# Last batch through masked 32-row groups, experts summed on VectorE, a semaphore per first load, new orders

## The chip, the cores and the metric

The kernel runs on one core of one Trainium2 chip. The metric is the device time in microseconds of one execution. Engines: PE (TensorE), DVE (VectorE), ACT (ScalarE), POOL (GpSimd), and SP (SyncE), which here issues the DMAs.

## The reference, cut to what matters

Eight batches of 256 tokens with 128 features pass four residual stages, each behind a layer norm:

```
x += tanh(g_xattn[0]) * attention(LN(x), ctx; 8 heads of 64, 512 keys) @ Wo + bo        stage X
x += tanh(g_ffn[0]) * (self-attention(LN(x); 16 heads of 8, 256 keys)
                       + top-2 of 8 experts, softmax gates, with biases)                stage F
x += tanh(g_xattn[1]) * attention(LN(x), ctx; 16 heads of 8, 512 keys) @ Wo + bo        stages K (keys, values), B
x += tanh(g_ffn[1]) * sum over top-2 experts of (x We + prob) * weight                  stage C
```

## The kernel before

Every batch is the same list of steps, named stage, step, batch, part. Stage X: xin and ctx (loads), ls, rs, xh (the norm: statistics on DVE, power on POOL, scaling on DVE), ln (transposes), kp, qp, vp (projections), mx (8 score fills, whose maxima DVE reduces), mT (the maxima as a row), e (8 exponent fills: scores again, minus the row maximum, exp on ACT), pv (times values), dn and dT (denominators), out (projection by Wo), xs (POOL sums the heads). Stages F and B, with heads of 8 rows: qk (projection), sp (POOL splits each f32 into three bf16 parts), sw and sr (the parts go to DRAM and come back restacked, 48 rows for each head, two heads side by side in row halves 0 to 63 and 64 to 127), mx8 (maxima; 8 fills for F, 16 for B), mT8, mw and mr (the maxima go through DRAM too, as a 49th row), e8 (8 and 16 fills), pv8, oT, and for B aT and out8 (Wo). F and C also have gate, gx (top 2 and weights w), moe (4 fills of 512 columns, times w on DVE, added up on POOL) and fin (POOL); the bias part of F is wT, wb. C ends with out, the store.

A fill is a PE step into one or two of eight PSUM banks that ACT or DVE then drains. The planner, `schedule()` (lines 256 to 322), lists all steps with costs and what they depend on, and chooses one greedily at a time by EARLY x start time + a wanted time (`AMOUNTS`, lines 51 to 93). Its result is `ORDER`, one fixed sequence for each engine; each engine executes its own, and waits on semaphores. `MODE` puts PE steps in groups that split the array alike; a change of group has a cost in the plan. `WARMERS` is a number of filler matmuls that the planner puts ahead of a PE step where it expects PE to idle (line 596: ident times wqx). `L...` in a profile is a line of this file.

What the change touches: the first loads (list `first`, line 499, one semaphore w_first of 8 x 16; awaited by PE at line 586, by ACT ahead of the Tanh at 757, by POOL at 1014); the 19 later loads (`loads`, semaphore w_loaded); the DVE memset of PSUM (833); POOL's memsets of k8 and v8 (1013); the steps of batch 7 in F, K, B and C; the planner. Lines that the prediction names: 601 ln, 605 qp, 609 kp, 620 and 706 scores for mx and mx8, 636 and 640 e, 649 pv, 667 out, 725 e8, 737 pv8, 693 moe on PE and 980 on DVE, 1069 to 1077 moe on POOL, 1085 to 1093 fin, 902 xh, 1027 and 1028 rs, 949 oT, 875 w.

Of the kernel before, what the change touches and what calls it, by code (L numbers as in the profile page):

```python
# [50 lines left out]
EARLY, SWITCH, PERIOD = 297.1242, 52.68, 114.223  # L51
AMOUNTS = {
# [13 lines left out]
    ("DVE", "C", "gate"): (273.74, -377.36), ("DVE", "C", "gx"): (98.96, 88.96), ("DVE", "C", "moe"): (-499.91, -524.03),  # L66
    ("POOL", "X", "rs"): (-116.96, 345.46), ("POOL", "X", "xb"): (-243.12, -152.43), ("POOL", "X", "e"): (82.49, 251.41),
    ("POOL", "X", "xs"): (114.49, -8.85), ("POOL", "F", "rs"): (162.64, -182.35), ("POOL", "F", "sp"): (-2.47, 375.02),
    ("POOL", "F", "moe"): (162.93, -42.41), ("POOL", "F", "fin"): (62.3, 335.36), ("POOL", "K", "sp"): (367.67, -161.62),
    ("POOL", "B", "rs"): (64.61, 155.9), ("POOL", "B", "xb"): (99.7, -174.62), ("POOL", "B", "sp"): (6.72, -89.93),  # L70
    ("POOL", "C", "rs"): (-194.63, 117.07), ("POOL", "C", "moe"): (290.04, 342.6), ("POOL", "C", "fin"): (650.19, -128.95),
# [1057 lines left out]
```

## Time and profile before

| | us |
|---|---|
| median of 3 runs | 736.36 (733.67 to 737.97) |
| the profiled execution | 737.18 |
| its span, first to last instruction | 735.3 |
| mean granted TensorE clock | 0.984 |
| PE, DVE, ACT, POOL busy | 649.0, 520.3, 401.1, 401.2 |

The span is what the rows below cut up; the profiled execution took 1.9 us more. Busy time is a union over instructions, and says of PE only that something was in the array, fillers included. A row of the timeline has start, duration, engine, line, operation, written tile and read tiles, and in brackets the idle time before it with what ended it.

### The profile page before, as it was taken

How to read it: one execution, taken by the hardware profiler on the slowest of the kernel's cores; microseconds unless marked ns; L12 is line 12 of the kernel's file. 1: busy time of each engine (PE TensorE's matmuls, PEld its weight loads, DVE VectorE, ACT ScalarE, POOL GpSimd, SP SyncE). 2: the span in 40 equal slices, each digit the busy share in tenths (PEclk: the TensorE clock that was granted, in tenths of full speed). 3: DMA queues.
4: the chain of work that ended last, by engine and by line, in shares of the span. 5: the costliest groups of instructions: out<-in, count | busy, mean ns of one | idle time of the engine just before them, and what ended most of it. 6: DMA issues, size and time to landing. Idle time of an engine off the chain costs nothing.

```text
span 735.3 us, 14119 instructions
## 1 busy us (share of the span) xinstructions
PE 649.0 (88%) x5616; PEld 338.8 (46%) x5616; DVE 520.3 (71%) x993; ACT 401.1 (55%) x562; POOL 401.2 (55%) x551
## 2 busy tenths in 40 slices
PE   3998997899899999999999998999999897897882
PEld 1564453554345533554454544554364444343541
DVE  2607557698758787897869787897778658958513
ACT  2463547456845675458655784558543861573350
POOL 7275784771575567628565566636663685040234
PEclk9999999999999999999999999999999999999898
DMA  6130324410060045102350046104420434210000
GB/s 184 40 71 18 75 44 65 98 45 2 9 139 3 12 95 104 44 12 68 78 98 2 20 95 115 28 14 86 89 48 12 89 81 111 44 45 8 2 8 8
DMA packets 64369, 40.62 MB, mean 55 GB/s; under 512 B 5032, under 2 KB 62320, under 8 KB 64304
## 3 DMA queue, kind: packets, MB, share of 16 engines
q1 hardware_dynamic: 64304, 39.72, 25.2%
q8 instruction: 44, 0.72, 0.4%
q14 instruction: 21, 0.17, 0.1%
HBM read 22.80 MB, written 16.91 MB: 54 GB/s over the span
## 4 chain that ended last, share of the span: by engine, by line
PE 54%; DVE 21%; POOL 8%; ACT 8%; issue 5%; DMA 2%; SPq 1%; POOLq 0%; DVEq 0%
PE psum L737 9%; PE psum L649 8%; PE psum L636 7%; DVE mx8B L992 7%; DVE mxA L917 3%; ACT probB L825 3%; PE psum L706 3%; PE psum L609 3%; PE psum L725 3%; PE psum L693 3%; PE psum L614 2%; ACT probX L806 2%; PE psum L700 2%; PE psum L640 2%; PE psum L596 1%
## 5 line engine op out<-in xcount | busy, mean ns | idle before, releaser
L992 DVE TENSOR_REDUCE mx8B<-psum 128x2 f32<-128x1024 f32 x128 | 148.3, 1215 | 13.7 <-PE psum L706 13.2
L825 ACT ACTIVATE probB<-psum 128x1024 f32<-128x1024 f32 x128 | 125.7, 1026 | 18.1 <-PE psum L725 17.6
L917 DVE TENSOR_REDUCE mxA<-psum 128x2 f32<-128x1024 f32 x64 | 76.7, 1217 | 35.2 <-PE psum L620 35.0
L806 ACT ACTIVATE probX<-psum 128x1024 f32<-128x1024 f32 x64 | 65.4, 1026 | 49.0 <-PE psum L640 48.7
L987 DVE TENSOR_REDUCE mx8F<-psum 128x4 f32<-128x1024 f32 x64 | 75.8, 1219 | 11.0 <-PE psum L700 10.0
L636 PE MATMUL psum<-qA,kA 64*128 64x256 f32 x512 | 76.9, 393 | 0.6 <-ACT mrow L779 0.5
L825 ACT ACTIVATE probF<-psum 128x1024 f32<-128x1024 f32 x64 | 63.4, 1023 | 16.9 <-PE psum L725 16.0
L1048 POOL TENSOR_TENSOR sums<-sums,probX 128x512 f32<-128x512 f32 x32 | 40.6, 1270 | 56.8 <-ACT probX L806 55.5
L737 PE MATMUL psum<-probB,v8B 128*9 128x256 f32 x1024 | 64.1, 393 | 4.6 <-ACT probB L825 2.8
L649 PE MATMUL psum<-probX,vX 128*64 128x256 f32 x512 | 62.1, 385 | 2.4 <-ACT probX L806 2.4
L706 PE MATMUL psum<-k8B,q8B 48*128 48x512 bf16 x256 | 47.2, 388 | 12.0 <-DVE mx8B L992 6.9
L1045 POOL TENSOR_TENSOR sums<-probX 128x512 f32<-128x512 f32 x32 | 40.6, 1268 | 19.2 <-ACT probX L806 19.1
L725 PE MATMUL psum<-q8B,k8B 49*128 49x256 bf16 x512 | 47.2, 274 | 3.0 <-ACT probB L825 2.0
L636 PEld LDWEIGHTS psum<-qA,kA 64*128 64x128 f32 x512 | 40.0, 189 | 17.8 <-issue 3.1
L649 PEld LDWEIGHTS psum<-probX,vX 128*64 128x64 f32 x512 | 34.0, 136 | 25.7 <-ACT probX L806 7.0
L1069 POOL TENSOR_TENSOR prodC<-prodC 128x256 f32<-128x256 f32 x32 | 23.3, 727 | 41.2 <-DVE prodC L980 41.0
L609 PE MATMUL psum<-cTX,wkx 96*128 96x512 f32 x64 | 34.5, 665 | 10.9 <-DMA wvx<-in_wvx 10.9
L1049 POOL TENSOR_TENSOR sums<-sums,probX 128x512 f32<-128x512 f32 x32 | 40.7, 1271 | 2.5
L737 PEld LDWEIGHTS psum<-probB,v8B 128*9 128x9 f32 x1024 | 25.6, 92 | 34.8 <-issue 6.1
L725 PEld LDWEIGHTS psum<-q8B,k8B 49*128 49x128 bf16 x512 | 17.5, 94 | 50.4 <-ACT probB L825 16.0
L1053 POOL TENSOR_TENSOR sums<-sums 128x512 f32<-128x512 f32 x16 | 20.3, 1268 | 33.5 <-DVE sums L926 33.5
L737 PE MATMUL psum<-probF,v8F 128*9 128x256 f32 x512 | 33.6, 380 | 3.7 <-ACT probF L825 2.7
(203 smaller groups left out, 1262.3 us busy)
## 6 DMA issues: line engine op xcount, KB each, us to landing
k8B<-k_dK SPq DMA_DIRECT2D x16, 384.0 KB, 6.0
k_dK<-partsK SPq DMA_DIRECT2D x8, 384.0 KB, 2.6
q8F<-q_dF SPq DMA_DIRECT2D x16, 192.0 KB, 4.5
k8F<-k_dF SPq DMA_DIRECT2D x16, 192.0 KB, 5.1
q8B<-q_dB SPq DMA_DIRECT2D x16, 192.0 KB, 3.8
k_dK<-partsK SPq DMA_DIRECT2D x8, 256.0 KB, 2.9
cTX<-in_ctxT SPq DMA_DIRECT2D x8, 192.0 KB, 2.7
cTK<-in_ctxT SPq DMA_DIRECT2D x8, 192.0 KB, 3.1
```

The source lines that it names most:

```text
L609: last = mm(ps[:, j * KV:(j + 1) * KV], wkx[:, (2 * k + j) * P:(2 * k + j + 1) * P], cT["X"][:], start=True, stop=True)
L636: mm(ps[:, 512 * i + SEQ * c:512 * i + SEQ * (c + 1)], kA[half_i, h, (2 * f + c) * P:(2 * f + c + 1) * P], qA[half_i, h, :], start=True, s ...
L649: last = mm(ps[64 * i:64 * i + 64, 0:SEQ], vX[:, c, h * XD:(h + 1) * XD], prob[s][(2 * k + c // 2) % SLOTS[s]][:, o:o + SEQ], start=(c == ...
L706: last = mm(ps[:, KV * i:KV * (i + 1)], q8[s][b % TURNS[s]][64 * i:64 * i + KROWS, p, t * P:(t + 1) * P], k8[s][b % TURNS[s]][64 * i:64 * ...
L725: last = mm(ps[:, 512 * i + SEQ * c:512 * i + SEQ * (c + 1)], k8[s][b % TURNS[s]][64 * i:64 * i + MROWS, p, (c0 + c) * P:(c0 + c + 1) * P] ...
L737: last = mm(ps[32 * i:32 * i + D8 + 1, 0:SEQ], v8[s][:, c, h, :], prob[s][(NPAIR * KEYS[s] // SEQ * b + u) % SLOTS[s]][:, o:o + SEQ], star ...
L806: nc.scalar.activation(prob[s][k % SLOTS[s]][:], ps, ACT.Exp, scale=float(XD) ** -0.5).then_inc(done["ACT"], 1)
L825: nc.scalar.activation(prob[s][(units * b + k) % SLOTS[s]][:], ps, ACT.Exp, scale=float(D8) ** -0.5).then_inc(done["ACT"], 1)
L917: nc.vector.tensor_reduce(mxA[:, t, h:h + 65:64], ps.rearrange("p (i n) -> p i n", i=2), AX.X, ALU.max, negate=True).then_inc(drained, 1)
L987: nc.vector.tensor_reduce(mx8[s][:, :, 2 * k:2 * k + 2].rearrange("p t i -> p i t"), ps.rearrange("p (i t n) -> p i t n", i=2, t=QT), AX.X ...
L992: nc.vector.tensor_reduce(mx8[s][:, t, 2 * p:2 * p + 2], ps.rearrange("p (i n) -> p i n", i=2), AX.X, ALU.max, negate=True).then_inc(drain ...
L1049: engine.tensor_tensor(sums[:, h], sums[:, h], p[:, :, 1, :], ALU.add).then_inc(S["X"]["psum"], 1)
```

## The change

1. First loads. wkx, ident and the gates are issued from ACT's queue, the rest from SP's, with a semaphore for each of ident, wkx, wqx, wvx, wox, graw and bo. Each step waits for what it reads. PE starts with 4 filler matmuls on mxA, once the first PSUM bank is cleared. The memsets of k8 and v8 become a planned POOL step `sets`; at its end it waits for w_loaded (20 loads now) and multiplies the masks with two biases. The bias scaling and pick become steps too (`bo`, `pick`).
2. Batch 7 of F and B. No split, no DRAM. The weights of the projections are loaded into wqx and wkx (`tw`). q is masked by head, so that of each group of 32 rows only 8 rows of one head are not zero; k stays as it is. tmx multiplies groups of 32 rows in bf16 for the maxima; tmT transposes these; te multiplies in f32, plus a bf16 product that subtracts the maxima, as e of stage X does. tpv, oT as before with heads in another sequence. qk becomes tqb (DVE, 4 masked copies), tqf (ACT, 4) and tkb (ACT, 2). POOL clears the tiles for it (`tset`).
3. Batch 7 of X: xs of part 1 runs on DVE (txs). Batch 7 of C: DVE multiplies and adds each of 8 experts from the banks (tmoe, 16 operations of 128 columns), POOL adds the bias part to x meanwhile (`tx`), DVE ends with tfin, and each half is stored by itself.
4. `AMOUNTS` and the greedy choice are gone. `TURN_OF` spells the sequence of each engine, a letter for each step (an index into STEPS); `schedule()` only derives banks, waits and fillers from it.

```diff
-START = 13.
+START = {"PE": 5.4, "DVE": 5.2, "ACT": 5.0, "POOL": 1.3, "SP": 9.0}
+EARLY_FILLERS = 4
-EARLY, SWITCH, PERIOD = 297.1242, 52.68, 114.223
-AMOUNTS = {
...
+STEPS = {
...
+    "POOL": (("X", "rs"), ("X", "pick"), ("X", "bo"), ("K", "sets"), ("X", "xb"), ("X", "e"), ("X", "xs"), ("F", "rs"),
...
+TURN_OF = {
+    "PE": "ebaycbdydddxdeddxdafgggghghbgggchihjkdkdbddededlddnmpofpggbgqpghggaphhsgsgssshssbsitcedjkukdurduvudduvueuvldumdv"
...
+    "POOL": "dacebalffffffffggehijfafffjffffjjkggehlimajfnojffjfjffffkggheimjjjjkonfalfpfffffqqfqmggheqriojjfpnffjfjffakfflqq"
...
+def plan_direct(p, s, b, keys, v, old):
+
+    n = KEYS[s] // P
+    units = GROUP * n
+    for k in range(units):
+        p.fill("DVE", 1, s, "tmx", b, k, .22, 1.13, [("DVE", s, "tqb", b, 0), keys], [("POOL", "F", "tset", b, 0)])
+        if k % n == n - 1:
+            p.fill("ACT", 0, s, "tmT", b, k // n, .22, .3, [("DVE", s, "tmx", b, k)], [("POOL", "F", "tset", b, 0)])
...
         @block.sync
-            load_x(0)
             load_ctx("X", 0)
-            for dst, src in first:
-                engine.dma_start(dst, src).then_inc(w_first, 16)
+            load_x(0)
+            engine.dma_start(wqx[:], a["wqx"]).then_inc(loaded["wqx"], 16)
+            engine.dma_start(wvx[:], a["wvx"]).then_inc(loaded["wvx"], 16)
+            for dst, src in bias:
+                engine.dma_start(dst, src).then_inc(loaded["bo"], 16)
+            engine.dma_start(wox[:], a["wox"]).then_inc(loaded["wox"], 16)
             for dst, src in loads:
                 engine.dma_start(dst, src).then_inc(w_loaded, 16)
-            sp.wait_ge(c_set, MEMSETS)
...
         @block.tensor
-            pe.wait_ge(w_first, W_FIRST)
+            pe.wait_ge(c_set, X_SETS)
             pe.wait_ge(ps_set, 1)
+            for _ in range(EARLY_FILLERS):
+                early = mm(psum[:, 0, 0:SEQ], mxA[:, 0, :], mxA[:].rearrange("p t n -> p (t n)"), start=True, stop=True)
...
+                elif name == "te":
+                    j, i, c0 = (k // 2, k % 2, 0) if s == "F" else (k // 4, k // 2 % 2, 2 * (k % 2))
...
+                    for c in range(2):
+                        for g in (2 * i, 2 * i + 1):
+                            o, rows = 512 * (g % 2) + SEQ * c, slice(ROWS * g, ROWS * g + ROWS)
+                            mm(ps[:, o:o + SEQ], keyL[s][rows, (c0 + c) * P:(c0 + c + 1) * P], qA[rows, j, :],
+                               start=True, stop=False, tile_position=(ROWS * g, 0))
+                        for g in (2 * i, 2 * i + 1):
+                            o, rows = 512 * (g % 2) + SEQ * c, slice(ROWS * g, ROWS * g + ROWS)
+                            last = mm(ps[:, o:o + SEQ], onesL[rows], rowL[j][rows], start=False, stop=True, tile_position=(ROWS * g, 0))
...
         @block.vector
+                if name == "tfin":
+                    dve.wait_ge(based, QT)
+                    dve.wait_ge(*is_done("C", "tmoe", b, 2 * k + 1))
+                    nc.vector.scalar_tensor_tensor(out=fin["C"][:, k, :], in0=acc["C"][:, k, :], scalar=gates[:, 3:4],
+                                                   in1=x1["C"][:, k, :], op0=ALU.mult, op1=ALU.add).then_inc(S["C"]["fin"], 1)
...
+                elif name == "tmoe":
...
+                    for e in range(4):
+                        part, weight = ps[:, e * P:(e + 1) * P], w[s][:, t, 4 * f + e:4 * f + e + 1]
+                        if f == 0 and e == 0:
+                            ins = nc.vector.tensor_scalar(acc[s][:, t, :], part, weight, None, ALU.mult)
+                        else:
+                            ins = nc.vector.scalar_tensor_tensor(out=acc[s][:, t, :], in0=part, scalar=weight, in1=acc[s][:, t, :],
+                                                                 op0=ALU.mult, op1=ALU.add)
+                        if e < 3:
+                            link(s, ins)
+                    ins.then_inc(drained, 1)
...
         @block.gpsimd
+                elif name == "sets":
+                    for tile in (*k8["F"], *k8["B"], v8["F"], v8["B"]):
+                        engine.memset(tile[:], 1.0).then_inc(k_set, 1)
+                    pool.wait_ge(w_loaded, W_LOADS)
+                    for to, n in (("F", 0), ("B", 2)):
+                        engine.tensor_scalar(bqm[to][:], mask[:], bqn[:, n:n + 1], None, ALU.mult).then_inc(k_set, 1)
```

The first letters on PE read: e vp, b kp, a ln, y vv of stage K, c qp, b kp, d mx. On POOL: d `sets`, a rs, c `bo`, e xb, b pick.

## Rows read from the trace of the kernel before

**Rows 1.** The page: span, busy time (share) xinstructions, and PE's busy tenths by slice.
```profile
span 735.3 us, 14119 instructions
PE 649.0 (88%) x5616; PEld 338.8 (46%) x5616; DVE 520.3 (71%) x993; ACT 401.1 (55%) x562; POOL 401.2 (55%) x551
...
PE   3998997899899999999999998999999897897882
```
**Rows 2.** Timeline of PE, 574:590: the last output projection of batch 7.
```profile
576.36 1.07 PE L667 MATMUL psum<-wox,oX 64*128 64x128 f32 x16
```
**Rows 3.** Timeline of all engines, 0:30.
```profile
9.98 0.59 POOL L1013 MEMSET v8B<- 128x576 f32 x1
...
10.90 3.78 PE L609 MATMUL psum<-cTX,wkx 96*128 96x512 f32 x4 [10.90 <-DMA wvx<-in_wvx]
...
14.02 0.43 SPq L556 DMA_DIRECT2D weB<-in_weB  x1
14.26 0.23 POOL L1027 TENSOR_SCALAR veX<-mvX 128x2 f32<-128x2 f32 x1
...
15.99 0.69 PE L601 MATMUL psum<-ident,xhX 128*128 128x128 f32 x2 [1.30 <-DVE xhX L902]
...
19.89 2.83 PE L605 MATMUL psum<-xTX,wqx 128*128 128x256 f32 x8
...
24.75 0.61 PE L620 MATMUL psum<-kAb,qAb 64*128 64x512 bf16 x4 [0.31 <-ACT qA L791]
```
**Rows 4.** Windows: length, busy of PE, PEld, DVE, ACT, POOL (x), PEclk, DMA share, GB/s.
```profile
287.70:368.70 81.00, 75.70 (x690) 39.42 (x690) 65.61 (x125) 49.88 (x71) 48.66 (x68) 1.00 0.27 58
...
577.50:647.70 70.20, 59.68 (x522) 30.05 (x518) 54.47 (x121) 34.09 (x52) 31.15 (x53) 1.00 0.38 76
647.70:711.00 63.30, 54.05 (x495) 26.38 (x494) 34.12 (x80) 34.72 (x47) 18.99 (x38) 0.92 0.07 18
```
**Rows 5.** Waits of PE, 287.7:529.6: us in total, times, longest.
```profile
PE psum L601 <- DVE xhB L902: 3.4, 3, 1.1
PE psum L693 <- DVE prodC L980: 3.1, 3, 1.1
```
**Rows 6.** Groups by line of PE, 577.5:711: busy us, mean ns, idle before.
```profile
L596 PE MATMUL psum<-wqx,ident 128*128 128x256 f32 x70 | 19.4, 426 | 2.1 <-DVE x L935 1.0 <-DVE mx8B L992 0.9 <-DVE v8B L960 0.2
```
**Rows 7.** Timeline of all engines, 704:736.
```profile
709.01 1.92 PE L737 MATMUL psum<-probB,v8B 128*9 128x256 f32 x32 [0.32 <-ACT probB L825]
...
712.48 0.29 DVE L949 TENSOR_TENSOR attB<-psum,rrB 128x128 f32<-128x128 f32 x1
...
723.40 0.17 DVE L875 TENSOR_TENSOR wC<-w0C,w1C 128x16 f32<-128x16 f32 x1
...
732.30 0.72 POOL L1093 TENSOR_TENSOR accC<-accC,x 128x256 f32<-128x256 f32 x1
```
**Rows 8.** Windows of 15 to 19 us, columns as in rows 4.
```profile
15.00:16.00 1.00, 0.01 (x1) 0.01 (x1) 0.60 (x2) 1.00 (x2) 0.30 (x1) 1.00 0.40 76
17.00:18.00 1.00, 1.00 (x2) 0.34 (x1) 0.00 (x0) 0.10 (x1) 0.00 (x0) 1.00 1.11 368
...
18.50:19.00 0.50, 0.50 (x1) 0.02 (x1) 0.00 (x0) 0.00 (x0) 0.00 (x0) 1.00 0.13 26
```
**Rows 9.** Timeline of PE, 391:402 and 655:704.
```profile
392.96 0.60 PE L636 MATMUL psum<-qA,kA 64*128 64x256 f32 x4
...
393.51 0.60 PE L636 MATMUL psum<-qA,kA 64*128 64x256 f32 x4
...
394.24 0.39 PE L706 MATMUL psum<-k8B,q8B 48*128 48x512 bf16 x2
394.62 1.95 PE L649 MATMUL psum<-probX,vX 128*64 128x256 f32 x16
396.50 0.39 PE L706 MATMUL psum<-k8B,q8B 48*128 48x512 bf16 x2
396.72 0.38 PE L725 MATMUL psum<-q8F,k8F 49*128 49x256 bf16 x4
...
663.47 3.58 PE L737 MATMUL psum<-probB,v8B 128*9 128x256 f32 x32 [0.30 <-ACT probB L825]
```

More of the change, by code:

```diff
@@ L50 @@
 IDLE, WARM_UP, WARM = .25, .43, True
-EARLY, SWITCH, PERIOD = 297.1242, 52.68, 114.223
-AMOUNTS = {
[13 rows of a table removed]
[L66 to L71, printed above, removed]
[21 rows of a table removed]
+LETTERS = "abcdefghijklmnopqrstuvwxyzABCDEFGHIJKLMNOPQRSTUVWXYZ0123456789"
@@ L157, in plan_gate @@
     for k, us in enumerate(busy):
-        p.job("DVE", s, "gx", b, k, us, ("ACT", s, "gx", b, 0), ("DVE", s, "moe", b - 1, 3), ("POOL", s, "fin", b - 1, 0))
+        p.job("DVE", s, "gx", b, k, us, ("ACT", s, "gx", b, 0), ("DVE", s, "moe", b - 1, 3), ("POOL", s, "fin", b - 1, 0),
+              *([("PE", "F", "wT", b - 1, 0)] if s == "F" else []))
 def plan_moe(p, s, b, last, old):
@@ L224, in plan_c, with turns @@
 def plan_c(p, b):
-    plan_norm(p, "C", b, ("DVE", "B", "out8", b, 0), [("PE", "C", "moe", b - 1, 3)])
+    plan_norm(p, "C", b, [("DVE", "B", "out8", b, 0)], [("PE", "C", "moe", b - 1, 3), ("PE", "C", "gate", b - 1, 0)])
     plan_gate(p, "C", b, (.8, .6, .6, .67))
-    plan_moe(p, "C", b, 3, ("SP", "C", "out", b - 1, 0))
-    p.job("SP", "C", "out", b, 0, .43, ("POOL", "C", "fin", b, 0))
+    if b < LAST:
+        plan_moe(p, "C", b, 3, ("SP", "C", "out", b - 1, 0))
+        p.job("SP", "C", "out", b, 0, .43, ("POOL", "C", "fin", b, 0))
+        return
+    p.job("POOL", "C", "tx", b, 0, 2.4, ("DVE", "C", "gx", b, 3), ("DVE", "C", "xh", b, 0))
+    for k in range(4):
+        p.fill("DVE", 0, "C", "tmoe", b, k, .86, 1.1, [("ACT", "C", "ln", b, 0)], [("DVE", "C", "gx", b, 3), ("SP", "C", "out", b - 1, 0)])
+    for k in range(QT):
+        p.job("DVE", "C", "tfin", b, k, .25, ("DVE", "C", "tmoe", b, 2 * k + 1), ("POOL", "C", "tx", b, 0))
+        p.job("SP", "C", "out", b, k, .43, ("DVE", "C", "tfin", b, k))
 def slack(key):
+    if key in (("SP", "X", "xin", 0, 0), ("SP", "X", "ctx", 0, 0)):
+        return 0.
     return OUT if key[0] == "PE" else LAND[key[1:3]] if key[0] == "SP" else 0.
-def targets(jobs):
-    count = {}
-    for e, s, name, b, k in jobs:
-        count[e, s, name] = max(count.get((e, s, name), 0), k)
-    out = {}
-    for key in jobs:
-        group, b, k = key[:3], key[3], key[4]
-        off, step = AMOUNTS[group]
-        out[key] = PERIOD * b + off + step * (k / count[group] if count[group] else 0.)
-    return out
+def turns(p):
+    groups, order = {}, {}
+    for key in p.jobs:
+        groups.setdefault(key[:3], []).append(key)
+    for e, letters in TURN_OF.items():
+        steps = [groups.pop((e, *group)) for group in STEPS[e]]
+        left = [iter(keys) for keys in steps]
+        order[e] = [next(left[LETTERS.index(letter)]) for letter in letters]
+        assert len(order[e]) == sum(len(keys) for keys in steps)
+    assert not groups
+    return order
 def free_banks(wide, bank_free, now):
@@ L261, in schedule @@
     jobs = {key: (busy, [a for a in after if a in p.jobs]) for key, (busy, after) in p.jobs.items()}
[L262 to L270 removed]
+    turn = turns(p)
+    free, at = dict(START), dict.fromkeys(turn, 0)
     never = 1e9
@@ L322, in schedule, with ready @@
-    return order, bank_of, before, p.drain, over, warm
+    over, before, warm = {}, {}, {}
+    def ready(key):
+        e, after = key[0], jobs[key][1]
+        if any(a not in over for a in after):
+            return None
+        return max([over[a] + HOP * (a[0] != e) for a in after], default=0.)
+    while len(over) < len(jobs):
+        went = False
+        for e in ("SP", "POOL", "ACT", "DVE"):
+            while at[e] < len(turn[e]) and ready(turn[e][at[e]]) is not None:
+                key = turn[e][at[e]]
+                free[e] = max(free[e], ready(key)) + jobs[key][0]
+                over[key] = free[e] + slack(key)
+                at[e] += 1
+                went = True
+                if p.drain.get(key[1:]) == e:
+                    for i in range(BANKS):
+                        if held[i] == key[1:]:
+                            bank_free[i] = over[key] + HOP
+        if went:
+            continue
+        key = turn["PE"][at["PE"]]
+        fill, other = key[1:], MODE.get(key[1:3], 0) != mode
+        start = max(free["PE"] + DRAIN_OUT * other, ready(key))
+        when, banks = free_banks(p.wide[fill], bank_free, start)
+        assert when < never
+        start = max(start, when)
+        idle = start - max(free["PE"], when)
+        warm[fill] = int(min(20, max(0., idle - IDLE) // WARM_UP)) if WARM else 0
+        before[fill] = [held[i] for i in banks if held[i]]
+        bank_of[fill] = banks[0]
+        for i in banks:
+            held[i], bank_free[i] = fill, never
+        free["PE"] = start + jobs[key][0]
+        if other:
+            mode = MODE.get(key[1:3], 0)
+            free["PE"] += ENTRY.get(key[1:3], .1)
+        over[key] = free["PE"] + slack(key)
+        at["PE"] += 1
@@ L325 @@
+    return {e: [key[1:] for key in keys] for e, keys in turn.items()}, bank_of, before, p.drain, over, warm
 ORDER, BANK, FORMER, DRAIN, OVER, WARMERS = schedule()
@@ L689, in _ @@
                         last = mm(ps[:, t * NE:(t + 1) * NE], xT[s][:, t * P:(t + 1) * P], wg[s][:], start=True, stop=True)
[L690 removed]
+                elif name in ("moe", "tmoe"):
                     t, f = divmod(k, 2)
```

415 lines of the change are left out of this document (293 added, 122 removed), and 54 rows, old and new, of tables (AMOUNTS, STEPS).

## The prediction

> **What bounds the kernel now.** The page comes first [rows 1]. TensorE (PE) is busy for 649.0 of 735.3 us, VectorE for 520.3, ScalarE and GpSimd for 401 each. The PE row has two soft ends: nothing in the first slice, and 7s and 8s in the last third. To give them sizes I cut the span at two events: the last matmul of the output projection of batch 7, at 577.4 us, and the last attention-times-value matmul of batch 7, which ends at 710.9 [rows 2, 7]. This gives four stretches.
>
> - Start: PE does nothing until 10.90, where it is released by wvx, last of the eight first loads. The first score matmul starts at 24.75 [rows 3].
> - Middle: three whole periods take 241.9 us, with some 75.6 us of PE work in each (the first is shown, 75.70 in 81.00) [rows 4]. PE is 94% busy, VectorE 81%. The waits that a profile can name sum to 14.0 us in the three periods, and the longest is 1.1 us [rows 5]. So the middle is bound by PE; only those some 5 us of idle per batch can be had there.
> - Tail, 577.5 to 711: 133.5 us, PE "busy" 59.68+54.05=113.7 [rows 4]. But 19.4 of it are filler matmuls that multiply ident by wqx and whose result nobody reads [rows 6]. Real work is 94.3 us, idle and filler 39.2 us. Here the round trips of the last batch through DRAM are no longer covered by other batches.
> - End chain, 711 to 735.3: 24.3 us of one dependent chain, oT, aT, out8, norm, gate, experts, store. From w at 723.57 on it alternates between DVE and POOL until the sum ends at 733.02 [rows 7].
>
> **The change part by part.**
>
> *First loads.* PE, ScalarE and the bias code no longer wait for all eight first loads. One would subtract the 10.9 us. I don't, because of the new GpSimd order: its first letter is d, the step `sets`, ahead of a, the step `rs` of batch 0. `sets` runs the memsets (the last starts at 9.98 before [rows 3]) and then waits for w_loaded, all 20 later loads, to make two masked biases. Queued behind this on POOL is rs, so xh, ln, qp and every score of batch 0 wait for the last weight load. When does it land? weB, the last of them, is issued at 14.02 [rows 3]; the DMA engines are full in 17:18 (1.11) and nearly idle (0.13) from 18.5 on [rows 8]; so the loads are in by about 18.3. In after, weB is SP's 27th issue and not its 29th, at 0.47 us each (29 issues up to 14.02, the first at 0.7): 0.95 us earlier, 17.3. DMA share was only 0.40 at 15:16 [rows 8], so issue, not the rate, sets the time there.
> The Trainium skill ("DMA: Bandwidth & Descriptors", section "Issuing engines are not separate DMA queues") says that issuing from several engines saves only the sequencer's time, because all run on the same 16 DMA engines. By that alone, with saturated engines, nothing lands earlier and the start would be 0.95 us worse than below; the share of 0.40 says that the engines had room.
> From 17.3, with durations of [rows 3]: two small bias operations 0.5, ve and rstd 1.03 (14.26 to 15.29), xh to first transpose 0.65, transposes at the idle clock 0.73 to the start of xT, xT 0.38. That is 20.6. The new PE order puts vv of batch 0 ahead of qp: about 0.7 later; qp 2.83, copies 2.0 (from the end of qp, 22.72, to 24.75): 26.2 against 24.75. kp and vp lie in PE's idle time in both, so the start costs **+1.4**. Bounds: -1 (loads land by 15, nothing ahead of qp) to +3.
>
> *Orders of batches 0 to 6.* Same steps, other sequence. I count mode groups along the PE order as the diff writes it out (groups of MODE): 371 changes of group instead of 339 up to the last output projection. A change costs 0.16: at 394.24 a pair that takes 0.22 elsewhere (396.50 to 396.72) is followed by the other mode only at 394.62 [rows 9]. 32 x 0.16 = +5.1. Against it stands the wait of L693 for prodC, 3.1 us in three periods, about 1.0 per batch [rows 5]. Before, the first three moe fills of C stand next to each other (1, 1 and 12 places apart), while GpSimd still adds up the products of the one before; in the new order they are 3 to 20 places apart. That wait goes: 7 x -1.0 = -7. The wait for xhB (also 1.1 each) stays, since the work between oT and ln of B is as long as before. Sum **-2**. Bounds: all 5 us per batch of idle gone, 6 x -5 + 5 = -25; as much new idle as was saved, +12. I take the small one because only one wait can be shown to go.
>
> *Last batch, attention of F and B.* Removed: the splits on POOL, the stores and loads of parts, maxima through DRAM. With them goes the reason for fillers and idle. Added on PE: each of the 24 exponent units was 4 bf16 matmuls, 0.22 like the score pair from 396.50 on, and is now 4 f32 and 4 bf16, like a unit of X, whose half takes 0.55 (392.96 to 393.51) [rows 9]: 24 x (1.09-0.22) = +20.9. Row transposes and the extra projections +2.2. Mode changes in the tail 111 instead of 82, as 32-row and 64-row units alternate: 29 x 0.16 = +4.6. Real work 94.3+27.7=122. Minus some 4 us (an estimate from the mean clock of 0.92 over 63.30 us) that cold stretches cost before (the 32 matmuls that take 1.92 at 709.01 take 3.58 at 663.47, in a stretch whose granted clock is 0.92 on average, so partly at 1.2 GHz and not 2.4 [rows 4, 7, 9]) = 118. The new order leaves no planned filler in the tail before the last ln. At the middle's share of 0.94: 126 us against 133.5, **-7.5**. What hides the added work is thus the idle and filler of 39 us, and only that. DVE has 24 reductions as before, plus two masked queries of 4 x 0.3 to 0.4 (128x128 from PSUM is 0.29, the nearest [rows 7]): +3 in a stretch where it is busy 88.6 of 133.5 [rows 4]; it doesn't take over. Bounds: idle share 0.02 gives 120; 0.14, as in 0.86 busy before, gives 137.
> The Trainium skill ("TensorEngine Tiling (Array Packing)", section "Tiling Modes") says that changing the tiling mode drains the TensorE, which speaks against alternating 32-row and 64-row units. It gives no price; the sum uses 0.16 from the row, and at ten times that the 29 changes would cost 46 us.
> The xs of row tile 1 moves from POOL to DVE (txs): F's norm starts about 3 us earlier. PE has other work there, so nothing.
>
> *End chain.* Up to w the chain is the same. Then, before, 9.46 us from 723.57 to 733.02 [rows 7]. After: 16 dependent DVE operations of 128x128 from PSUM and two fin. 0.29 for such an operation [rows 7] plus 0.05 for the link: 16 x 0.34 + 2 x 0.25 = 5.9. POOL's `tx` (about 2 us, started at w) is ready before the first fin. **-3.6**. Bounds: 0.25 each, 4.5 (-5); 0.45 each if in1 from SBUF slows it, 7.7 (-1.8). The last store is half as large, at most -0.2.
>
> **Sum.** 735.3 +1.4 -2 -7.5 -3.6 = 723.6 span; the profiled execution took 737.2, 1.9 more than its span, so 725.5; the median of the runs lies 0.8 below it: **724.7 us**.
>
> **Rivals.**
> - *The start is worth its full size.* If rs isn't held by the loads (w_loaded landing by 11), rs goes at 10.8 behind the memsets and the first score at about 18.5: 6.3 earlier than before, not 1.4 later. 717. Against: the order of POOL, which can be read.
> - *The new orders win half of the idle of the middle*, 2.5 us more per batch: 15 us less, 710. For: VectorE has 19% to spare and the waits are many and short. Against: only one of them is seen to be addressed.
> - *Idle moves, not goes.* The tail runs at 0.86 busy and the middle gains nothing: 137 and 0, so 737: same as before. For: the sequences fit the durations that the plan assumes, and these are off where a load is waited for: it gives `sets` 9.8 us, and by the working above it ends 6 us later.
> - *Slower:* 32-row f32 units don't overlap in pairs. A unit of 1.09 us then takes 2.0 and more; 24 x 0.95 = +23, of which at most the 8 us of leftover idle hide: about 740. It decides from about 1.6 us per unit: then the 13 us of gain are gone. For: no 32-row contraction is in the trace. Against: pairs of 64 rows overlap, the first pair of f32 matmuls and its bf16 pair together 0.55 [rows 9]. The same side is reached if the middle's new orders cost 3 us a batch.
>
> **How the numbers follow.** Forecast and near it (715 to 732) 0.54; full start or better middle (700 to 715) 0.18; idle moved (732 to 741) 0.17; slower than that 0.11. For 8 in 10 I leave out some of both ends: 706 to 741. About 0.5%, 3.7 us, is what a measurement can tell from no change. Below 732.7: 0.54+0.18 and a little of the next, 0.74. Within 732.7 to 740: 0.13. Above: 0.13.
>
> **What would show it.** Right: POOL's rs of batch 0 starts after 17 us, with idle before it released by a weight load; first score matmul at 25 to 27. Periods of 79 to 81 us. In the last 145 us L596 under 4 us busy, and te units at 1.09. From w to the last fin 5.9 us. Wrong: first score before 20; periods under 78 or over 82; te units over 1.2; PE idle of more than 1 us for DVE in the tail, which would make VectorE the bound there.

## The result, and the profile after

The changed kernel takes **729.03 us** (median of 4 runs, 725.92 to 733.98), the kernel before beside it 737.16 (733.67 to 738.88). The ratio is 0.9896 with a 95% interval of 0.9849 to 0.9943: 1.0% less time, clear of the scatter, if not by much. Predicted was 724.7 with a range of 706 to 741. Measured once more with the experiments below, the same kernel gave 726.58 (722.62 to 730.74), ratio 0.9868 [0.9827, 0.9910].

The profiled execution took 733.98 us and is the longest of the first four. It differs from the others mainly in the clock that TensorE was granted: their spans and mean clocks are 724.1 at 0.986, 726.9 at 0.979, 727.6 at 0.975 and 732.2 at 0.968. The profiled execution of the second measurement took 725.35 us (span 723.6, clock 0.980). Both are shown.

The page of after, first rows, as in [rows 1], and then its PE row by slices with the granted clock below it:

```profile
span 732.2 us, 14403 instructions
PE 666.7 (91%) x5766; PEld 347.3 (47%) x5766; DVE 515.4 (70%) x1018; ACT 402.4 (55%) x574; POOL 385.8 (53%) x535
...
PE   6898998998989899988999998999999999999984
...
PEclk9899999999898999989999999999999989999998
```

The holes in the last third of the PE row are gone; PE is busy for 17.7 us more and the span is 3.1 shorter. Of the 17.7 us, 7.1 lie in the start and 6.8 in the middle, by the windows below. The cuts are those of the prediction, at the first score matmul, the last output projection of batch 7 and the last attention-times-value matmul, first for before, then after, then after measured again. Columns: stretch, length, busy time of PE, PEld, DVE, ACT, POOL (instructions), granted clock, DMA share, GB/s.

```profile
0.00:24.75 24.75, 12.23 (x23) 5.79 (x24) 5.99 (x13) 7.75 (x10) 14.83 (x20) 1.00 0.50 137
24.75:577.50 552.75, 513.70 (x4542) 270.75 (x4542) 417.05 (x744) 323.18 (x452) 327.57 (x423) 0.99 0.26 55
577.50:711.00 133.50, 113.72 (x1016) 56.43 (x1012) 88.59 (x201) 68.80 (x99) 50.14 (x91) 0.96 0.24 48
711.00:735.30 24.30, 9.33 (x40) 5.79 (x40) 8.63 (x36) 1.36 (x4) 8.63 (x18) 0.86 0.02 6
```
```profile
0.00:27.41 27.41, 19.34 (x49) 12.73 (x50) 6.08 (x13) 6.67 (x8) 15.40 (x22) 0.81 0.46 124
27.41:585.10 557.69, 520.46 (x4542) 270.28 (x4542) 405.97 (x746) 322.08 (x455) 325.57 (x422) 0.98 0.25 54
585.10:710.40 125.30, 117.56 (x1138) 58.47 (x1138) 91.15 (x209) 72.27 (x108) 38.70 (x76) 0.96 0.10 24
710.40:732.20 21.80, 9.35 (x43) 5.79 (x40) 12.19 (x50) 1.37 (x4) 6.12 (x17) 0.86 0.04 12
```
```profile
0.00:26.63 26.63, 19.28 (x48) 12.65 (x48) 5.92 (x13) 6.66 (x8) 15.40 (x22) 0.81 0.48 128
26.63:579.30 552.67, 516.62 (x4541) 268.62 (x4542) 406.21 (x746) 322.27 (x455) 325.57 (x422) 0.99 0.25 55
579.30:701.90 122.60, 114.44 (x1138) 57.59 (x1138) 91.20 (x209) 72.29 (x109) 38.60 (x77) 0.99 0.10 25
701.90:723.60 21.70, 9.34 (x40) 5.79 (x40) 12.19 (x50) 1.34 (x4) 6.10 (x16) 0.87 0.04 12
```

| stretch | before | predicted | after, first | after, again |
|---|---|---|---|---|
| start | 24.75 | +1.4 | +2.7 | +1.9 |
| middle | 552.75 | -2 | +4.9 | -0.1 |
| tail | 133.5 | -7.5 | -8.2 | -10.9 |
| end | 24.3 | -3.6 | -2.5 | -2.6 |
| span | 735.3 | -11.7 | -3.1 | -11.7 |

The two executions of one program differ by 8.6 us, 5.0 of it in the middle and 2.7 in the tail. PE is busy in the middle for 3.8 us more with the same matmuls: a difference of granted clock (0.98 and 0.99), not of work.

*Start.* Timeline of after, all engines, to be read beside [rows 3]:

```profile
9.98 0.58 POOL L1259 MEMSET v8B<- 128x576 f32 x1
...
17.77 0.32 POOL L1262 TENSOR_SCALAR bqmF<-mask,bqn 128x4 f32<-128x4 f32 x1 [7.21 <-DMA weB<-in_weB]
...
18.33 0.23 POOL L1273 TENSOR_SCALAR veX<-mvX 128x2 f32<-128x2 f32 x1
...
19.40 0.65 DVE L1073 TENSOR_SCALAR xhX<-xin,mvX,rstdX 128x128 f32<-128x128 f32 x2 [13.42 <-POOL rstdX L1274]
...
20.20 0.66 PE L692 MATMUL psum<-ident,xhX 128*128 128x128 f32 x2 [3.06 <-DVE xhX L1073]
...
20.66 1.06 PE L826 MATMUL psum<-wv8B,cTK 96*128 96x128 f32 x4
...
21.51 3.67 PE L697 MATMUL psum<-xTX,wqx 128*128 128x256 f32 x8
...
27.41 0.39 PE L714 MATMUL psum<-kAb,qAb 64*128 64x512 bf16 x2
```

This is the chain that the prediction read from the order of POOL: the memsets end at 10.56, then 7.21 us of nothing until weB lands, and rs behind it at 18.33.

*Middle.* Waits of PE, 27:585 (total, times, longest), to be read beside [rows 5]; and the first matmul behind each of the two longest:

```profile
PE psum L772 <- DMA cTK<-in_ctxT: 3.5, 1, 3.5
PE psum L847 <- DMA q8B<-q_dB: 3.3, 1, 3.3
```
```profile
218.16 2.08 PE L772 MATMUL psum<-cTK,wk8B 96*128 96x512 f32 x2 [3.54 <-DMA cTK<-in_ctxT]
...
315.28 0.61 PE L847 MATMUL psum<-k8B,q8B 48*128 48x512 bf16 x2 [3.28 <-DMA q8B<-q_dB]
```

Over the whole middle, the wait for prodC went from 4.2 us before to 0.7, as predicted. The wait for xhB went too, from 5.5 to 0.2, which was predicted to stay. In their place PE waits for two DMAs, once each. The waits of PE that the profile can name add up to 37.1 us before and still to 34.9. Behind each of the two DMA waits the granted clock falls, in windows of after:

```profile
218.00:225.00 7.00, 6.84 (x36) 3.83 (x36) 2.42 (x3) 2.56 (x4) 0.00 (x0) 0.56 0.33 76
315.00:323.00 8.00, 7.65 (x52) 4.03 (x54) 4.71 (x4) 1.44 (x3) 2.22 (x5) 0.70 0.01 2
```

*Tail.* Groups by line of PE, 585:711. No row of the filler's line (686) is left in it, against 19.4 us in [rows 6]. The largest group of new work is that of te (24 exponent units, two float32 records for each product):

```profile
L803 PE MATMUL psum<-qA,kA 32*128 32x256 f32 x192 | 26.8, 397 | 1.6 <-ACT probB L983 1.0 <-DVE mx8B L1225 0.4 <-ACT probB L996 0.2
```

*End.* Timeline from w on, beside the last two of [rows 7]: w at 722.89, the first sum ends at 726.28, the second at 729.76, the last fin at 730.15.

```profile
722.89 0.17 DVE L1047 TENSOR_TENSOR wC<-w0C,w1C 128x16 f32<-128x16 f32 x1
...
723.54 2.74 DVE L1212 SCALAR_TENSOR_TENSOR accC<-psum,wC,accC 128x128 f32<-128x128 f32 x7
...
724.39 1.20 POOL L1333 TENSOR_SCALAR x<-x,cb 128x128 f32<-128x128 f32 x2
726.39 0.35 DVE L1094 SCALAR_TENSOR_TENSOR accC<-accC,gates,x 128x128 f32<-128x128 f32 x1
```

### The profile page after: what moved, and what is told of

It is laid out like the page before. It is cut to its first block, busy times and chain, and to the rows that moved or that the text cites. A ratio compares the mean times of both kernels' runs of the same rounds, so it can differ in the third digit from the quotient of the medians.

```text
span 732.2 us, 14403 instructions
## 1 busy us (share of the span) xinstructions
PE 666.7 (91%) x5766; PEld 347.3 (47%) x5766; DVE 515.4 (70%) x1018; ACT 402.4 (55%) x574; POOL 385.8 (53%) x535
## 4 chain that ended last, share of the span: by engine, by line
PE 53%; DVE 26%; ACT 6%; POOL 5%; DMA 4%; issue 3%; SPq 1%; DVEq 0%; POOLq 0%; ACTq 0%
PE psum L878 7%; PE psum L730 6%; PE psum L743 5%; DVE mx8B L1225 5%; DVE mx8F L1220 5%; PE psum L834 5%; PE psum L866 4%; DVE mxA L1105 3%; PE psum L847 2%; PE psum L702 2%; PE psum L803 2%; PE psum L708 2%; ACT probB L996 2%; PE psum L815 2%; PE psum L761 1%
## 5 line engine op out<-in xcount | busy, mean ns | idle before, releaser
L1225 DVE TENSOR_REDUCE mx8B<-psum 128x2 f32<-128x1024 f32 x112 | 131.6, 1216 | 15.1 <-PE psum L847 14.2
L996 ACT ACTIVATE probB<-psum 128x1024 f32<-128x1024 f32 x112 | 110.7, 1028 | 25.5 <-PE psum L866 19.9
L1220 DVE TENSOR_REDUCE mx8F<-psum 128x4 f32<-128x1024 f32 x56 | 66.2, 1219 | 21.9 <-PE psum L841 21.5
L996 ACT ACTIVATE probF<-psum 128x1024 f32<-128x1024 f32 x56 | 56.7, 1026 | 21.1 <-PE psum L866 17.8
L878 PE MATMUL psum<-probB,v8B 128*9 128x256 f32 x896 | 56.0, 392 | 0.3 <-ACT probB L996 0.2
L866 PE MATMUL psum<-q8B,k8B 49*128 49x256 bf16 x448 | 43.6, 284 | 5.2 <-ACT probB L996 2.1
L847 PE MATMUL psum<-k8B,q8B 48*128 48x512 bf16 x224 | 41.2, 384 | 6.0 <-DMA q8B<-q_dB 3.3
L734 PE MATMUL psum<-mrow,pick 64*128 64x256 bf16 x256 | 35.8, 271 | 0.0
L878 PEld LDWEIGHTS psum<-probB,v8B 128*9 128x9 f32 x896 | 22.4, 92 | 28.1 <-issue 6.7
L866 PEld LDWEIGHTS psum<-q8B,k8B 49*128 49x128 bf16 x448 | 15.5, 97 | 42.5 <-ACT probB L996 12.8
L834 PE MATMUL psum<-weF,xTF 128*128 128x512 f32 x64 | 34.6, 622 | 0.8 <-ACT probB L996 0.5
```

Of the source, the lines that this page charges most:

```text
L834: last = mm(ps, xT[s][:, t * P:(t + 1) * P], we[s][:, f * 512:(f + 1) * 512], start=True, stop=True)
L847: last = mm(ps[:, KV * i:KV * (i + 1)], q8[s][b % TURNS[s]][64 * i:64 * i + KROWS, p, t * P:(t + 1) * P], k8[s][b % TURNS[s]][64 * i:64 * ...
L866: last = mm(ps[:, 512 * i + SEQ * c:512 * i + SEQ * (c + 1)], k8[s][b % TURNS[s]][64 * i:64 * i + MROWS, p, (c0 + c) * P:(c0 + c + 1) * P] ...
L878: last = mm(ps[32 * i:32 * i + D8 + 1, 0:SEQ], v8[s][:, c, h, :], prob[s][(NPAIR * KEYS[s] // SEQ * b + u) % SLOTS[s]][:, o:o + SEQ], star ...
L996: nc.scalar.activation(prob[s][(units * b + k) % SLOTS[s]][:], ps, ACT.Exp, scale=float(D8) ** -0.5).then_inc(done["ACT"], 1)
L1220: nc.vector.tensor_reduce(mx8[s][:, :, 2 * k:2 * k + 2].rearrange("p t i -> p i t"), ps.rearrange("p (i t n) -> p i t n", i=2, t=QT), AX.X ...
```

## The experiments

All are edits of the changed kernel, measured beside the kernel before on the same chip. Medians of the kernel before were 737.2, 737.9 and 736.3 in the three groups (the first four experiments, the next four, the last three). Each group ran on another chip, so across groups the ratios are the safer comparison.

**1. Old orders in the middle (h_mid).** The sequences of all engines up to the last output projection of batch 7 are those of the kernel before, with the changed kernel's tail and end.

```
 TURN_OF = {
-    "PE": "ebaycbdydddxdeddxdafgggghghgbgg...   "SP": "abgaghbibacdefacdjbkeflh...
+    (the letters of before's ORDER up to X out of batch 7, then those of after)
```

> The changed kernel, but the engines follow the sequences of the kernel before up to the end of batch 7's output projection (the start keeps POOL's memsets and load wait ahead of rs), then the new ones. Theory O (the new middle orders themselves cost the 5 us by which the middle grew, 552.7 to 557.7 us from the first score matmul to that projection): the middle comes back to 552 to 554, PE waits for cTK and q8B of 3.5 and 3.3 us are gone, total 722 to 725. Theory C (the orders are neutral, the profiled execution only met more low-clock stretches): middle 553 to 558 at any clock, total as the changed kernel, 727 to 731. Theory of the prediction (orders save 2): total 730 to 732. Tail under all of them: 125 us from that projection to the last attention-times-value matmul.

Measured: 724.39 us (723.72 to 727.37), ratio 0.9836 [0.9810, 0.9862]. Span 722.6 at a clock of 0.988; middle 551.3, tail 123.5. Window and waits of PE for its middle:

```profile
26.10:577.40 551.30, 512.41 (x4542) 269.55 (x4546) 417.64 (x746) 323.48 (x452) 326.60 (x422) 1.00 0.24 56
...
PE psum L692 <- DVE xhB L1073: 5.4, 5, 1.1
PE psum L834 <- DVE prodC L1197: 4.2, 4, 1.1
```

The waits of [rows 5] are back, those for cTK and q8B are gone, and the kernel is no slower than with the new orders; its median lies 2.2 and 4.6 below the two of the changed kernel. So the new orders of batches 0 to 6 bring nothing as they stand, which is what theory O expected (722 to 725). The gain of the change, 8 to 11 us, comes from the tail and the end.

**2. The start: mask biases off `sets` (s_bqm).** The wait for the 20 loads and the two multiplications go from `sets` to `tset`, a step of batch 7.

```
                 elif name == "sets":
                     ...
-                    pool.wait_ge(w_loaded, W_LOADS)
-                    (two bqm multiplications)
                 elif name == "tset":
+                    pool.wait_ge(w_loaded, W_LOADS)
+                    (two bqm multiplications)
...
-                sp.wait_ge(k_set, K_SETS)          (and the same on DVE)
+                sp.wait_ge(k_set, K_SETS - 2)
```

> The changed kernel; only the two masked-bias products and their wait for the 20 later loads move from the end of POOL's step sets to tset in batch 7. Theory S (POOL's wait for the loads holds the start): rs starts at 10.6 and not 18.3; qp then waits for vv alone, which also waits for the loads, so the first score matmul comes at 24 to 25 and not 27.4: total 3 us less, 726. Rival (the time at the start is taken by the cold array and the DMA, not by that wait): first score at 27, total 729.

Measured: 723.14 us (722.10 to 727.29), ratio 0.9813 [0.9786, 0.9841]. Timeline of its start:

```profile
10.63 0.23 POOL L1273 TENSOR_SCALAR veX<-mvX 128x2 f32<-128x2 f32 x1
...
17.86 0.38 PE L692 MATMUL psum<-ident,xhX 128*128 128x128 f32 x2
...
18.90 1.89 PE L697 MATMUL psum<-xTX,wqx 128*128 128x256 f32 x8
```

rs starts 7.7 us earlier, but the transposes only 2.3, because PE first works off its own queue: fillers from 9.10 on, vp at 14.43, kp at 16.15. qp takes 1.89 and not 3.67. The first score comes at 22.82, 4.6 earlier, and the time falls by 3.4 against the kernel measured again (5) and 5.9 against the first result, so theory S holds. The start of the changed kernel is held as the prediction says; behind that hold stands PE's order.

**3. The start in full (s_full).** As 2, and for batch 0 rs is first on POOL, ln and qp stand behind the first kp on PE, vv goes behind the scores, and the planned fillers of batch 0 are left out.

```
+WARMERS.update({fill: 0 for fill in WARMERS if fill[2] == 0})
-    "PE": "ebaycbdydddxdeddxdaf...   "POOL": "daceb...
+    "PE": "bacbedddeddxdydydaf...    "POOL": "acedb...
```

> As s_bqm, and nothing of batch 0 that needs the 20 later loads stands ahead of a score any more: POOL does rs, bias, xb and only then the memsets; PE kp, ln, qp, kp, vp, then scores, with kk and vv behind the fifth; no fillers in batch 0. Theory S: first score matmul at 14 to 16 and not 27.4, and since the middle is bound by PE nearly all of it is kept: 716 to 719. Rival R (the later loads return as a wait: kk, vv and the restacked keys are needed by then, so what is gained is lost by batch 1): start gains 12, total only 3 to 5 less, 724 to 726.

Measured: 719.87 us (716.26 to 721.32), ratio 0.9769 [0.9743, 0.9796]. rs at 6.08, first score at 15.04. Windows of start and middle:

```profile
0.00:15.04 15.04, 11.06 (x30) 6.27 (x31) 4.86 (x8) 6.92 (x9) 8.40 (x14) 1.00 0.68 172
15.04:570.20 555.16, 518.87 (x4556) 270.71 (x4555) 407.15 (x751) 321.76 (x455) 331.98 (x429) 0.99 0.26 56
```

The first score is 12 us earlier than in after, as expected; of this some 7 to 9 reach the end (by the medians), and the time is 0.9 above the bracket of theory S. The middle is 2.5 longer than in the second profile of after (555.2 and 552.7), since steps that lay in the start lie there now.

**4. One read earlier on SP (d_ksr).** The read of B's restacked keys of batch 2 (K sr) is issued ahead of F's stores of batch 3. In after SP issues it at 302.59, behind the four reads for F and directly ahead of the queries q8B, at 303.84.

```
-    "SP": "...hmacjdngikbeflm...
+    "SP": "...hmaicjdngkbeflm...
```

> The changed kernel with one step moved: on SP the restacked keys of stage K, batch 2, are read ahead of the stores of F, batch 3, as before the change, and not together with the reads for F3 and B2. Theory Q (three reads in one burst queue behind each other on the DMA engines; PE then waits 3.3 us for q8B near 315 us and a low-clock stretch follows): that wait falls under 1 us, the low clock there goes, total 4 to 7 us less, 722 to 725. Rival (the time returns at the next wait, as VectorE and the orders are tight): wait gone, total within 2 of 729.

Measured: 721.89 us (719.15 to 728.77), ratio 0.9798 [0.9756, 0.9840]. q8B is issued at 299.46, and the wait for it is gone; that for cTK stays (first row: waits of PE):

```profile
PE psum L772 <- DMA cTK<-in_ctxT: 3.8, 1, 3.8
```
```profile
27.60:577.30 549.70, 514.35 (x4541) 267.97 (x4541) 406.01 (x746) 322.17 (x455) 325.66 (x422) 1.00 0.26 55
```

The middle is 3.0 shorter than in after measured again and 8.0 shorter than in the first profile. One letter of SP's order was worth more than the 2 us that the new orders of the middle had been predicted to bring. The trace shows the place: the same step w of VectorE comes 1.0 us later here than in 5 at 294.25, 2.1 earlier at 341.61, and 2.1 earlier at the end. So theory Q holds; that the queueing of the reads delayed q8B is argued from the order of issue. With this read moved, the new orders win 1.6 us of middle against the old ones (549.7 and 551.3).

**5. The changed kernel once more (ctrl)**, unchanged, as the base for the next three.

> The changed kernel itself, beside the three others of this job: 727 to 730 by all theories. Across its executions the span should follow the granted clock (theory C: about 4 us more span for each 0.01 less clock, as 724.1 at 0.986 and 732.2 at 0.968), and its lowest should stay near 724 when the clock is near 0.986.

Measured: 726.58 us (722.62 to 730.74), ratio 0.9868 [0.9827, 0.9910]. Its six runs in order of span: 720.8 at a mean clock of 0.985, 723.3 at 0.986, 723.6 at 0.980, 726.0 at 0.976, 727.2 at 0.975, 728.9 at 0.972. The scatter of this kernel goes with that of its clock, 4 to 6 us for 0.01 (8.1 for 0.013 here, 8.1 for 0.018 in the first four runs).

**6. The float32 product out of te (te_bf16).** The scores of the 24 masked exponent units are multiplied in bfloat16 only; this leaves accuracy out for batch 7.

```
-    mm(ps[:, o:o + SEQ], keyL[s][rows, ...], qA[rows, j, :],
+    mm(ps[:, o:o + SEQ], keyLb[s][rows, ...], qAb[rows, j, :],
```

> The changed kernel; the exponent units te of batch 7 take their scores from the bf16 copies of queries and keys, so one bf16 product stands in place of the f32 one (this leaves accuracy out for batch 7, otherwise all is computed). Theory P (the tail is bound by PE, so the 20.9 us of added f32 work were paid for out of idle time and the gain would have been larger without them): from batch 7's output projection to the last attention-times-value matmul 108 to 113 us and not 125, total 12 to 17 less than the unedited one. Rival V (VectorE's chain of 24 reductions and queries sets the tail): 120 to 125 us, total at most 4 less.

Measured: **733.94 us** (730.16 to 739.87), ratio 0.9969 [0.9936, 1.0003]. It fits no theory: with less to multiply the kernel is 7.4 us slower than 5. Windows of its tail, a place in it, and a group of its PE by line (columns of the group: count, busy, mean ns):

```profile
578.20:710.50 132.30, 116.82 (x1042) 52.38 (x1042) 91.15 (x209) 72.28 (x108) 37.65 (x75) 0.85 0.10 23
...
640.00:660.00 20.00, 19.71 (x144) 9.29 (x148) 9.76 (x42) 12.14 (x18) 4.98 (x9) 0.66 0.01 1
```
```profile
640.29 0.66 PE L692 MATMUL psum<-ident,xhC 128*128 128x128 f32 x2 [2.45 <-DVE xhC L1073]
...
642.03 2.08 PE L772 MATMUL psum<-cTK,wkx 96*128 96x512 f32 x2
```
```profile
L815 PE MATMUL psum<-probB,v8B 128*9 128x256 f32 x128 | 11.0, 503 | 0.7 <-ACT probB L983 0.7
```

The clock in the tail is 0.85 against 0.99. After 2.45 us of idle PE runs at the lower level: two matmuls of L772 take 2.08 us there and 1.12 in after at 646.23, where the same wait for xhC was 1.40 us. One long idle is not the only way down: in 630 to 635 the granted clock is 0.50 too, behind a stretch (625 to 630) in which PE was busy for 3.33 of 5 us and no wait was over 0.6. The attention-times-value matmuls take 503 ns on average (380 in 5). PE is busy for longer (116.8 and 114.4 us) with less to do.

**7. The end chain undone (c_pool).** Experts of the last C go back to products on DVE and sums on POOL.

> The changed kernel with the experts of the last batch as before: DVE multiplies 512 columns at a time, POOL adds up and does fin, one store. By the working of the prediction, corrected by the trace (from w to the last sum 7.1 us after and 9.5 before, one store of twice the size 0.2 more): the end chain from 711 on is 2.6 longer, total +2.5. Rival (in the chain the last store or POOL's tx is what ends last): total within 1 of the unedited one.

Measured: 730.86 us (726.81 to 733.45), ratio 0.9920 [0.9887, 0.9953]; 4.3 above 5. From w at 714.51 to the end of the last sum at 724.11 its trace has 9.6 us, against 7.3 in after; with the larger store the end stretch is 24.3 us, against 21.7 in 5. These 2.6 are what was expected. The intervals of 5 and 7 overlap, so the rest of the 4.3 is not settled.

**8. Start, earlier read and later kk (best).** As 3 and 4, and kk of batch 2 stands five PE steps later, so that cTK has landed.

> Three edits together: the start of s_full (12 us earlier first score), the read of K2 ahead of the stores of F3 on SP, and kk of batch 2 four fills later on PE (its load came 3.5 us late). Gains add if each is on PE's path: 719.9 less 5 to 7 for the read, less 2 to 3 for kk: 709 to 713. If they eat the same idle time: 715 to 719.

Measured: 720.42 us (718.35 to 721.89), ratio 0.9774 [0.9743, 0.9806]: no gain on 3, and above both brackets. The wait for cTK is gone, but its middle is 556.8. Experiment 11 has the same kernel without the later kk, and the two traces show where the time goes. The same step w of VectorE comes 2.8 us later here than there ahead of kk (193.78 and 191.03), 0.1 later behind it (245.95 and 245.83), and 6.8 later soon after 366 (429.86 and 423.05). So the later kk did win 2.6 us, and more was lost far behind it, at a vp of batch 5 (first row here, second in 11):

```profile
366.65 3.78 PE L709 MATMUL psum<-wvx,cTX 96*128 96x512 f32 x4 [1.84 <-ACT probB L997]
```
```profile
364.49 1.88 PE L709 MATMUL psum<-wvx,cTX 96*128 96x512 f32 x4
```

`schedule()` gives out the PSUM banks by the sequence, so moving one step gives 583 of 937 fills another bank. By its result this vp follows the last exponent fill of B of batch 2 in its bank, and in 11 an ln and a pv8. Behind the wait PE is granted 0.57 (366 to 374), and 1.00 in 11. That the new bank is the reason for the wait is read from plan and trace; no run tests it by itself.

**9. Half of the float32 work put back as ballast (te_half).** As 6, but the first half of each unit also does its float32 product, whose result is overwritten. Accuracy as in 6.

```
+    if c == 0:
+        mm(ps[:, o:o + SEQ], keyL[s][rows, ...], qA[rows, j, :], start=True, stop=True, ...)
     mm(ps[:, o:o + SEQ], keyLb[s][rows, ...], qAb[rows, j, :], start=True, stop=False, ...)
```

> te_bf16 replaced the float32 score product of the 32-row exponent units by a bfloat16 one and was 7 us slower than the changed kernel, with a mean granted clock of 0.962 and a tail of 132.4 us. Here the scores are again bfloat16, but half of the float32 matmuls are kept as work whose result is overwritten, so that TensorE's own work in these units (about 13.4 + 12.3 = 25.7 us) is what the changed kernel has (26.8). Theory: what was lost was the granted clock, because TensorE idled more; with the work put back the tail is 118 to 126 us, the stretch 620 to 700 is granted 0.95 or more, and the time is 722 to 728. Rival: something else of the bfloat16 copies (their making on ScalarE, their place in the order) delays the tail; then the tail stays at 129 or more and the time at 731 to 737. The scores of batch 7's masked units are of lower accuracy here.

Measured: 729.03 us (724.24 to 732.83), ratio 0.9896 [0.9854, 0.9938]. Windows of its tail, whole and in part:

```profile
579.20:703.70 124.50, 115.42 (x1138) 57.33 (x1138) 91.00 (x209) 72.46 (x109) 38.30 (x76) 0.95 0.10 24
```

The tail is 124.5 us (132.3 in 6, 122.6 in 5), its clock 0.95 (0.85, 0.99). By ratios 0.0073 of the 0.0101 that 6 had lost against 5 came back. The length of the tail is as the first theory expects. The clock came back in part: 620 to 700 is granted 0.91, where 0.95 or more was expected (0.77 in 6, 0.98 in 5). The median is 1 us above the bracket of the theory, and below the rival's. The intervals of 9 and 5 overlap.

**10. Old middle with the full start (best3).**

> The orders of the kernel before up to the last output projection of batch 7, as in h_mid, with the start of s_full (mask biases last on GpSimd, no wait for the last weight load, no warm-up matmuls in batch 0), and the changed kernel's tail and end. If the two gains add (h_mid 724.4, start 7 to 11 us): 713 to 717. If they don't, as in best, because an earlier start is given back in waits of the middle: 719 to 724. The longest waits of the middle are then again those for prodC and xhB, and none for cTK or q8B is over 1 us.

Measured: 717.15 us (715.66 to 721.62), ratio 0.9750 [0.9712, 0.9787]. The gains of 1 and 3 add, less some 2 us: its first score is at 17.25, not 15.04, and its middle is 553.4, not 551.3. PE's order up to the first score is that of 3; its qp takes 3.56 us there and 1.97 in 3, so the later start is one of clock.

**11. New middle with the full start and the earlier read (best2).**

> The changed kernel's orders with the start of s_full and the read of K2 issued before those of F3, as in d_ksr, without the later kk2 of best. If the gains add (s_full 719.9, d_ksr 4.7 us below the changed kernel): 713 to 717, and no wait for q8B. If it was the early start itself that made best lose elsewhere: 718 to 722, as best. The difference between the two readings is what best's later kk2 cost.

Measured: **716.46 us** (713.50 to 720.71), ratio 0.9728 [0.9692, 0.9765], the best of all, 2.7% below before. Its middle is 552.3 us, with the wait for cTK (3.7 us) and without the one at 366 of 8. 10 and 11 can't be told apart.

## Why the prediction was right, and where not

The sum was 723.6 us of span. The changed kernel spans 723.6 in one profile and 732.2 in another, its medians are 729.0 and 726.6. Sign and range held; the time is 2 to 4 us too low. That one span agrees to the tenth is luck: in that profile the tail gained 3.4 us more than forecast, and start, middle and end together 3.4 less.

- *The start, +1.4: +2.7 and +1.9.* The mechanism is shown by the rows above and by experiment 2: rs waits behind `sets` for weB. The load landed 0.5 us later than worked out. The rest is qp, taken as 2.83 and measured as 3.67; in experiment 2 the same eight matmuls take 1.89. So 3.67 is nearly all at the lower level and 2.83 partly. The window of before's start says 1.00, but its kp takes 3.78 us [rows 3] and 1.88 in experiment 2, so in the start the durations are the better witness. A duration from a row of before carries the clock of that row with it. That the start was worth its full size was a rival; it came true only when the order was changed, in experiments 3, 10 and 11. The Trainium skill ("DMA: Bandwidth & Descriptors", section "Issuing engines are not separate DMA queues") says that more issuing engines save only the sequencer's time. Experiment 3 doesn't contradict it: its edit touches no load, only fewer steps wait for the last one.
- *The middle, -2: +4.9 and -0.1.* **This step failed**, though not by much: its -7 for idle. The prodC wait went, as predicted, and the xhB wait besides. But idle and filler of PE together (fillers 3.45 us before, 1.20 after) went from 42.5 us to 37.3 in the second profile, 5.3 less and not 7, and 4.1 less in the first. In the first profile two new waits for DMA, 6.8 us together, take the place of the old ones. The prediction looked only at what PE, POOL and DVE do, and not at SP's order, in which the change moves reads against each other; and it took kk of batch 2 for a step like any other, though it reads a tile that a DMA refills. Experiment 4 shows the size for one of the two: 3.0 us of middle. For the other, experiment 8 shows 2.6 us won at its place. The rest of the +4.9 is PE's own work at a lower clock, 3.8 us between two executions of the same program.
- *Mode changes, 0.16 each.* A little dear at most. A half of a te unit takes 0.54 behind its own kind (682.25 to 682.79 in after) and 0.65 behind another mode, or ahead of one (632.75 to 633.39 to 634.04): 0.11 per change.

```profile
632.75 0.70 PE L803 MATMUL psum<-qA,kA 32*128 32x256 f32 x4
...
633.39 0.60 PE L803 MATMUL psum<-qA,kA 32*128 32x256 f32 x4
...
634.04 0.61 PE L847 MATMUL psum<-k8B,q8B 48*128 48x512 bf16 x4
```

  PE work in the middle, fillers left out, rose by 5.2 us from before to the second profile (510.25 to 515.42), where 5.1 had been set. Between experiments 1 and 4, whose middles are both granted 1.00, it is 4.2 us (508.95 and 513.15) for the same 32 changes, 0.13 each. The Trainium skill ("TensorEngine Tiling (Array Packing)", section "Tiling Modes") says that a change of mode drains the TensorE. The trace agrees that it costs something, 0.11 to 0.16 us a change. In the middle it ate nearly all that was saved in idle.
- *The tail, -7.5: -8.2 and -10.9.* Right, and the step that carries the result: experiment 1, which keeps the old orders up to the tail, has the whole gain. A unit takes 1.09 as forecast (two halves of 0.54), so the slower rival falls: 32-row products overlap in pairs. PE's share is 0.94 and 0.93, as assumed. The work is 114.4 us at a clock of 0.99, not 118. One of the signs of being wrong did show: PE idles 1.40 us for DVE (xhC, at 645.25). It is the only such wait, and VectorE is busy for 91 of 125 us, so it did not become the bound. What neither the prediction nor the expectation of experiment 6 saw is that this work can't be taken out for gain. The expectation subtracted most of 20.9 us; a unit with bf16 alone takes 0.46 (two halves of 0.23, from 625.74 on), so the edit removes 24 x (1.09 - 0.46) = 15 us of work. Removing it cost 7.4 us: PE then idles between dependent steps, and what it does next runs at 1.2 GHz. "Real work plus idle" is not additive in a stretch where both fit closely: the work sets the clock of the rest, as experiments 6 and 9 show for this tail.
- *The end, -3.6: -2.5 and -2.6.* Right mechanism (experiment 7), one term mis-sized: eight sums take from 723.16 to 726.28, 0.39 each and not 0.34, and a fin 0.35, not 0.25: 7.1 us in place of 5.9. POOL's `tx` was ready in time, at 725.59 against 726.28.
- *The rivals.* Not one holds as a whole. "Idle moves" is right about the middle, which gains nothing: two waits went and two others came. It is wrong about the tail, where PE is 0.94 busy and not 0.86.

What stays open: why one execution meets more stretches of low clock than another. Also, experiment 9 leaves 2 of 7 us between ballast and real products, which is within the scatter; half of the float32 work may not be enough, or the bfloat16 copies cost a little in themselves. An order in which cTK's load is issued earlier, without a later kk, was not tried.

## What to carry to other kernels

When a fixed order is rewritten, read the DMA queue's order as closely as those of the engines: one read behind others was worth 3 us here. One wait at the head of GpSimd's queue held the first score by 4.6 us, and PE's own order behind it by another 7.8. Where banks are given out by the sequence, a step that is moved can also make a wait far behind it, as at 366 us in experiment 8. A wait for "all loads" belongs in the step that needs them, not at the end of a step that happens to be early. And before work is taken off TensorE in a stretch of dependent steps, look at what it will do with the time: if it idles, the clock may take back more than the work cost.
